# A first attention's scores as three single-pass products, with the work of four engines reordered around them

## What is computed

```python
x = x + tanh(g_xattn[0]) * L0_xattn(layernorm(x), ctx, ctx, mask, Wq, Wk, Wv, Wo)   # 32 query heads, 8 key heads of 128, rope, capped logits
x = x + tanh(g_ffn[0])   * L0_ffn(layernorm(x), ...)      # base matrix, 4 active low-rank experts, softmax router
x = x + tanh(g_xattn[1]) * L1_xattn(layernorm(x), ...)    # 8 heads of 8 within patches of 128
x = x + tanh(g_ffn[1])   * L1_ffn(layernorm(x), ...)      # 8 experts of 512x512, the best 2 of each row
```

```python
q, k = apply_rope(q), apply_rope(k)
logits = 30 * tanh(einsum('btkgd,bTkd->bkgtT', q, k) * 0.0883883 / 30)
weights = softmax(where(mask, logits, -1e30)); attn = einsum(weights, v); return attn @ Wo
```

## Time and profile before

| | |
|---|---|
| median of 3 runs | 913.25 us (911.86 to 913.34) |
| the profiled execution, own time | 913.61 us |
| its span in the profile | 911.8 us |
| busy: TensorE, VectorE, GpSimd, ScalarE | 96%, 67%, 46%, 36% |
| the 8 groups of the first attention | about 43 to 608 us |
| the experts' tiles | about 815 to 897 us |

### The profile page before, as it was taken

How to read it: one execution, slowest core, us unless ns; L and a number is a source line. 1 busy time by engine, 2 the same in 40 slices (tenths; PEclk the granted TensorE clock), 3 DMA queues, 4 the chain that set the end, 5 groups by cost and what they waited for, 6 DMA issues and landing times.

```text
span 911.8 us, 13908 instructions
## 1 busy us (share of the span) xinstructions
PE 874.1 (96%) x4786; PEld 708.4 (78%) x4786; DVE 608.6 (67%) x1059; ACT 326.2 (36%) x590; POOL 416.9 (46%) x423
## 2 busy tenths in 40 slices
PE   6899999999999999999999999999999999998992
PEld 4777877887877897787897787778789999557881
DVE  5876576456576537557536656768899886869445
ACT  4424124204214222412421411423266678542331
POOL 4463153253163225235315316334898865828651
PEclk9999999999999999999999999999999999999996
DMA  9010120002012002012001100203155230763448
GB/s 322 21 58 36 35 72 21 12 15 79 1 62 66 1 12 92 0 35 92 0 12 46 47 1 1 83 1 117 46 145 153 74 78 10 278 239 118 162 159 313
DMA packets 42344, 71.02 MB, mean 78 GB/s; under 512 B 7082, under 2 KB 14827, under 8 KB 42099
## 3 DMA queue, kind: packets, MB, share of 16 engines
q1 hardware_dynamic: 37170, 58.00, 19.8%
...
...
## 4 chain that ended last, share of the span: by engine, by line
PE 89%; DVE 5%; issue 2%; DMA 1%; ACT 1%; POOL 1%; ACTq 1%; SPq 0%; DVEq 0%; POOLq 0%
PE ps L1423 19%; PE ps L1425 19%; PE ps L1424 19%; PE ps L1548 6%; PE ps L1540 6%; PE ps L1681 6%; PE ps L1556 3%; PE ps L1669 3%; PE ps L1662 2%; DVE w_lo L1283 1%; PE ps L1808 1%; PE ps L1752 1%; PE ps L1471 1%; PE ps L1433 1%; DMA y_in<-y_rows 1%
## 5 line engine op out<-in xcount | busy, mean ns | idle before, releaser
L556 POOL TENSOR_TENSOR q_t<-rot_a,rot_b 128x512 f32<-128x512 f32 x64 | 82.6, 1291 | 149.8 <-DVE rot_b L1003 149.8
L1423 PE MATMUL ps<-xt_hi,wq_hi 128*128 128x512 f32 x256 | 107.6, 420 | 3.2 <-DVE rot_b L1003 3.1
L1001 DVE TENSOR_TENSOR rot_a<-ps,cos 128x512 f32<-128x512 f32 x80 | 55.1, 689 | 83.1 <-PE ps L1425 82.4
L1423 PE MATMUL ps<-wo_hi,at_hi 128*128 128x512 f32 x256 | 106.7, 417 | 0.4 <-DVE at_lo L1118 0.4
L790 ACT ACTIVATE ps<-ps 128x512 f32<-128x512 f32 x64 | 37.2, 582 | 178.7 <-PE ps L1540 178.7
L1425 PE MATMUL ps<-xt_hi,wq_lo 128*128 128x512 f32 x256 | 101.1, 395 | 0.0
L1424 PE MATMUL ps<-xt_lo,wq_hi 128*128 128x512 f32 x256 | 101.0, 394 | 0.0
L1425 PE MATMUL ps<-wo_hi,at_lo 128*128 128x512 f32 x256 | 100.2, 391 | 0.0
L1424 PE MATMUL ps<-wo_lo,at_hi 128*128 128x512 f32 x256 | 99.8, 390 | 0.0
L803 ACT ACTIVATE at_hi<-ps 128x512 fp32r<-128x512 f32 x64 | 38.2, 597 | 171.6 <-PE ps L1556 171.6
L1123 DVE TENSOR_TENSOR X<-ps,X 128x512 f32<-128x512 f32 x64 | 44.2, 690 | 74.4 <-PE ps L1425 74.1
...
## 6 DMA issues: line engine op xcount, KB each, us to landing
wq_raw<-in_wq SPq DMA_DIRECT2D x8, 1024.0 KB, 5.5
wo_raw<-in_wo SPq DMA_DIRECT2D x8, 1024.0 KB, 5.1
w_raw<-in_we SPq DMA_DIRECT2D x8, 1024.0 KB, 6.7
...
q_t<-in_ctx_t SPq DMA_DIRECT2D x2, 1024.0 KB, 10.0
...
```

What stands on the lines that cost most here:

```text
L556: nc.gpsimd.tensor_tensor(dst, rot_a[:, r % 2, :], rot_b[:, r % 2, :], ALU.add).then_inc(rope_ok, 1)
L1001: nc.vector.tensor_tensor(heads(rot_a[:, r % 2, :]), heads(bank), bcast(cos[:, :], 4), ALU.mult)
L1423: nc.tensor.matmul(dst, w_hi, x_hi, start=start and k == 0, stop=False)
```

## The change

It does four things.
1. The scores become a `product` of rounded and remaining parts. New tiles `q_hi`, `q_lo`, `k_hi`, `k_lo`. ScalarE rounds each rotated tile (`turned_hi`, ten a group); the remainders are made half on VectorE (`turned_lo` for r = 0 to 4) and half on GpSimd (r = 5 to 9), in place, since `q_t` and `k_t` now lie where `q_lo` and `k_lo` are (`over` gives a tile the place of the one allocated next). To make room, `wo_raw` lies where `wo_lo` is, so `load_wo` waits for the last output of the group before, and `v_ones` is narrower.
2. The queues are reordered: on TensorE `output(1)` comes before `scores(4)`, and an output does its eight products of the rounded rows before it waits for the remainders; ScalarE, GpSimd and SP as the diff shows.
3. The count and route operations move from before group 0 to between group 6 and group 7.
4. The experts' products come in fours (rounded, remaining rows, remaining weights), each with its own wait.

The diff, cut to its core:

```diff
...
-wo_raw = sb("wo_raw", [P, G, D])
 wo_hi = sb("wo_hi", [P, G, D], F32R)
+wo_raw = over("wo_raw", [P, G, D])
 wo_lo = sb("wo_lo", [P, G, D], F32R)
-q_t = sb("q_t", [P, G, N])
-k_t = sb("k_t", [P, N])
-v_ones = sb("v_ones", [P, B, 2, P + 4])
+q_hi = sb("q_hi", [P, G, N], F32R)
+q_t = over("q_t", [P, G, N])
+q_lo = sb("q_lo", [P, G, N], F32R)
+k_hi = sb("k_hi", [P, N], F32R)
+k_t = over("k_t", [P, N])
+k_lo = sb("k_lo", [P, N], F32R)
+v_ones = sb("v_ones", [P, B, 2, P + 2])
 e_w = sb("e_w", [P, 2, G * P])
...
+def turned_tile(r, queries, keys):
+    if r < 2:
+        return keys[:, r * HALF:(r + 1) * HALF]
+    half, head = divmod(r - 2, G)
+    return queries[:, head, half * HALF:(half + 1) * HALF]
...
             load_wv(g // 2)
-        sp.wait_ge(wo_lo_ok, CREDIT + G * g)
-        load_wo(g)
         sp.wait_ge(qp_mm, CREDIT + 8 * g)
         load_wq(g)
+        sp.wait_ge(wo_mm, CREDIT + B * g)
+        load_wo(g)
...
         gp.wait_ge(rot_ok, CREDIT + 10 * g + r + 1)
-        if r < 2:
-            dst = k_t[:, r * HALF:(r + 1) * HALF]
-        else:
-            half, head = divmod(r - 2, G)
-            dst = q_t[:, head, half * HALF:(half + 1) * HALF]
-        nc.gpsimd.tensor_tensor(dst, rot_a[:, r % 2, :], rot_b[:, r % 2, :], ALU.add).then_inc(rope_ok, 1)
+        nc.gpsimd.tensor_tensor(turned_tile(r, q_t, k_t), rot_a[:, r % 2, :], rot_b[:, r % 2, :], ALU.add).then_inc(rope_ok, 1)
+    def turned_lo(g, r):
+        gp.wait_ge(sh_ok, CREDIT + 10 * g + r + 1)
+        lo_part(turned_tile(r, q_lo, k_lo), turned_tile(r, q_t, k_t), turned_tile(r, q_hi, k_hi), sl2_ok)
     def group(g, p, odd, last=False):
-        for r in range(2, 10):
+        for r in range(2, 8):
             rope_sum(g, r)
-            if r < 2 + G:
-                wo_split(g, r - 2)
+            if r == 5:
+                turned_lo(g, 5)
+            if r >= 5:
+                wo_split(g, r - 5)
+        wo_split(g, 3)
+        rope_sum(g, 8)
+        turned_lo(g, 6)
+        turned_lo(g, 7)
+        turned_lo(g, 8)
+        rope_sum(g, 9)
+        turned_lo(g, 9)
         if last:
...
     row_hi_first(1)
+    def turned_hi(g, r):
+        ac.wait_ge(rope_ok, CREDIT + 10 * g + r + 1)
+        hi_part(turned_tile(r, q_hi, k_hi), turned_tile(r, q_t, k_t), sh_ok)
...
     row_hi_first(7)
+    turned_hi(0, 0)
+    turned_hi(0, 1)
     def group(g, p, odd, last=False, first=False):
-        for k in range(G):
-            wo_split(g, k)
         if not odd and not first:
...
+        for k in range(G):
+            turned_hi(g, 2 + k)
+            wo_split(g, k)
+        turned_hi(g, 6)
         weights(0)
         weights(1)
+        turned_hi(g, 7)
         for b in range(B):
...
                 weights(b + 2)
+            if b < 2:
+                turned_hi(g, 8 + b)
             if last and b >= B - 2:
...
                 wv_split(p + 1)
+        if not last:
+            turned_hi(g + 1, 0)
+            turned_hi(g + 1, 1)
...
     ac.wait_ge(route_in, 32)
-    nc.scalar.activation(tri[:, :], tri_raw[:, :], ACT.Copy).then_inc(tri_ok, 1)
+    nc.scalar.activation(tri[:, :], tri_raw[:, :], ACT.Copy).then_inc(kz_ok, 1)
     ac.wait_ge(c2_mm, CREDIT + B)
...
     nc.vector.memset(count[:, 0, :], 0.0).then_inc(prep_v, 1)
-    step = 4
+    step = 5
     def rotate(g, r):
...
+    def turned_lo(g, r):
+        ve.wait_ge(sh_ok, CREDIT + 10 * g + r + 1)
+        nc.vector.tensor_tensor(turned_tile(r, q_lo, k_lo), turned_tile(r, q_t, k_t), turned_tile(r, q_hi, k_hi).bitcast(F32),
+                                ALU.subtract).then_inc(sl_ok, 1)
...
     turned_first(7)
-    ve.wait_ge(prep_v, CREDIT + step)
-    for k in range(4):
-        nc.vector.scalar_tensor_tensor(count[:, k + 1, :], iota[:, :], active_f[:, k:k + 1], count[:, k, :],
-                                       ALU.is_equal, ALU.add).then_inc(prep_v, 1)
-        ve.wait_ge(prep_v, CREDIT + step + k + 1)
-    step += 4
-    nc.vector.tensor_scalar(absent[:, :], count[:, 4, :], 0.5, BIG, ALU.is_gt, ALU.mult).then_inc(prep_v, 1)
-    ve.wait_ge(gates_ok, CREDIT + 1)
-    nc.vector.tensor_tensor(route_1[:, :], log_prior[:, :], rb[:, :], ALU.add).then_inc(prep_v, 1)
-    ve.wait_ge(prep_v, CREDIT + step + 2)
-    nc.vector.tensor_scalar(absent2[:, :], absent[:, :], -BIG, None, ALU.add).then_inc(prep_v, 1)
-    ve.wait_ge(prep_v, CREDIT + step + 3)
-    nc.vector.tensor_tensor(route_bias[:, :], route_1[:, :], absent2[:, :], ALU.add).then_inc(prep_v, 1)
+    turned_lo(0, 0)
+    turned_lo(0, 1)
     ve.wait_ge(prep_mm, CREDIT + 1)
     nc.vector.tensor_scalar(cap[:, :], ps[:, 7, 0:P], 0.5, TINY, ALU.is_lt, ALU.mult).then_inc(prep_v, 1)
-    ve.wait_ge(prep_v, CREDIT + step + 5)
+    ve.wait_ge(prep_v, CREDIT + step)
     nc.vector.scalar_tensor_tensor(cap[:, :], maskf[:, :], BIG, cap[:, :], ALU.mult, ALU.add).then_inc(cap_ok, 1)
...
-        for r in range(2, 8):
+        rotate(g, 2)
+        for r in range(3, 8):
             rotate(g, r)
+            if r < 6:
+                turned_lo(g, r - 1)
         mask(0)
...
         add(B - 1)
+        if not last:
+            turned_lo(g + 1, 0)
+            turned_lo(g + 1, 1)
...
         group(g)
+    ve.wait_ge(prep_v, CREDIT + step)
+    for k in range(4):
+        nc.vector.scalar_tensor_tensor(count[:, k + 1, :], iota[:, :], active_f[:, k:k + 1], count[:, k, :],
+                                       ALU.is_equal, ALU.add).then_inc(prep_v, 1)
+        ve.wait_ge(prep_v, CREDIT + step + k + 1)
+    step += 4
+    nc.vector.tensor_scalar(absent[:, :], count[:, 4, :], 0.5, BIG, ALU.is_gt, ALU.mult).then_inc(prep_v, 1)
+    ve.wait_ge(gates_ok, CREDIT + 1)
+    nc.vector.tensor_tensor(route_1[:, :], log_prior[:, :], rb[:, :], ALU.add).then_inc(prep_v, 1)
+    ve.wait_ge(prep_v, CREDIT + step + 2)
+    nc.vector.tensor_scalar(absent2[:, :], absent[:, :], -BIG, None, ALU.add).then_inc(prep_v, 1)
+    ve.wait_ge(prep_v, CREDIT + step + 3)
+    nc.vector.tensor_tensor(route_bias[:, :], route_1[:, :], absent2[:, :], ALU.add).then_inc(prep_v, 1)
...
         def scores(b):
-            if b in (0, 4):
-                pe.wait_ge(rope_ok, CREDIT + 10 * g + 6 + b)
+            if b == 0:
+                pe.wait_ge(sl_ok, CREDIT + 5 * g + 5)
+                pe.wait_ge(sl2_ok, CREDIT + 5 * g + 1)
+            if b == 4:
+                pe.wait_ge(sl2_ok, CREDIT + 5 * g + 5)
             pe.wait_ge(e_ok, CREDIT + B * g + b - 1)
-            nc.tensor.matmul(ps[:, 2 + b % 2, :], k_t[:, b * P:(b + 1) * P], q_t[:, :, b * P:(b + 1) * P],
-                             start=True, stop=True).then_inc(s_mm, 1)
+            rows = slice(b * P, (b + 1) * P)
+            product(ps[:, 2 + b % 2, :], [(k_hi[:, rows], k_lo[:, rows], q_hi[:, :, rows], q_lo[:, :, rows])]).then_inc(s_mm, 1)
...
                 pe.wait_ge(wo_lo_ok, CREDIT + G * (g + 1))
+            pe.wait_ge(ah_ok, CREDIT + B * g + b + 1)
+            pe.wait_ge(x1_ok, CREDIT + B * g + b)
+            for n in range(G):
+                rows = at_hi[:, b % 2, n * P:(n + 1) * P]
+                nc.tensor.matmul(ps[:, 7, :], rows, wo_hi[:, n, :], start=n == 0, stop=False)
+                nc.tensor.matmul(ps[:, 7, :], rows, wo_lo[:, n, :], start=False, stop=False)
             pe.wait_ge(al_ok, CREDIT + B * g + b + 1)
-            pe.wait_ge(x1_ok, CREDIT + B * g + b)
-            product(ps[:, 7, :], [(at_hi[:, b % 2, n * P:(n + 1) * P], at_lo[:, b % 2, n * P:(n + 1) * P],
-                                   wo_hi[:, n, :], wo_lo[:, n, :]) for n in range(G)]).then_inc(wo_mm, 1)
+            for n in range(G):
+                end = nc.tensor.matmul(ps[:, 7, :], at_lo[:, b % 2, n * P:(n + 1) * P], wo_hi[:, n, :], start=False, stop=n == G - 1)
+            end.then_inc(wo_mm, 1)
...
             weighted(b)
-            if b + 2 < B:
+            if b == 2:
+                output(1)
+                scores(4)
+            elif b + 2 < B:
                 scores(b + 2)
...
                 next_keys(0, KT // 2, KT)
-            output(b - 1)
+            if b != 2:
+                output(b - 1)
             turn(b)
...
-    pe.wait_ge(kz_ok, CREDIT + 1)
-    pe.wait_ge(tri_ok, CREDIT + 1)
+    pe.wait_ge(kz_ok, CREDIT + 2)
     pe.wait_ge(sel_ok, CREDIT + 1)
...
         e = pe.value_load(of_tile_i[0:1, i:i + 1], min_val=0, max_val=EX - 1)
+        bank = ps[:, 4 + i % 4, :]
+        if i < EX:
+            pe.wait_ge(weh_ok, max(hi_count(KT * own + KT - 1) for own in range(i + 1)))
+        pe.wait_ge(gh_ok, CREDIT + i + 1)
+        pe.wait_ge(r_ok, CREDIT + i - 3)
+        for k in range(KT):
+            nc.tensor.matmul(bank, gx_hi[:, i % 2, k, :], w_hi[:, bass.ds(e, 1), k, :], start=k == 0, stop=False)
+        pe.wait_ge(glo_ok, CREDIT + i + 1)
+        for k in range(KT):
+            nc.tensor.matmul(bank, gx_lo[:, i % 2, k, :], w_hi[:, bass.ds(e, 1), k, :], start=False, stop=False)
         if i < EX:
...
                 pe.wait_ge(wel_v, CREDIT + by_v)
```

(18 more changed lines are left out.)

## The result

The changed kernel takes 931.9 us (median of 4 runs, 930.2 to 935.5), the kernel before 913.3 (median of 4 beside them). The ratio is 1.017, with a 95% interval of 1.012 to 1.021. Forecast 940.4, range 919 to 945: slower, as said, by two thirds of what was said.

A forecast was written before the change was run, and what follows sets the result against it. TensorE, busy 874.1 of 911.8 us, was taken to bound the kernel. Eight groups at +3.45 give +27.6; with -0.8 and +0.9 at the edges and experts -0.9, +26.8 on 913.6 makes 940.4 us, range 919 to 945.

The forecast's parts named there:

- scores: Each score's matmuls on TensorE shrink from 0.86 to 0.69 us: 0.17 saved, 1.36 us a group.
- tile 4, tile 5: TensorE stalls before query tiles 4 and 5, waiting for late rotations on VectorE: 0.9 and 1.15 us a group.
- scores(0): TensorE waits at a group's first scores for GpSimd's subtraction turned_lo(5): 0.65 us stall.
- weighted(0): TensorE waits at a group's first weighted sum for mask(0): 0.85 us stall.
- output(1): Later rotation 9 and turned_hi(9) delay at_hi(1), so TensorE waits: 0.5 us a group (0 to 1.0).
- output(2): TensorE waits for add(1), queued on VectorE behind mask(4): 0.85 us a group.
- the price of `turned_lo` on VectorE: Each such subtraction right behind a rotation, as GpSimd's rope sum starts, takes 1.83 us; bounds 0.61 and 1.83.
- row 34.07: Profile row: a VectorE operation on SBUF, 0.05 us ahead of GpSimd's rope sum, takes 1.63 us, ending 0.28 behind it.
- the rule beside it: Trainium skill: VectorE and GpSimd share an exclusive port, first issuer keeps it; as rival, GpSimd waits: 928 us, chance 0.17.
- 828.37: Profile row: a VectorE subtraction taking 2.31 us, ending 0.56 behind GpSimd's own, which starts at 828.81.
- this branch of the forecast: Main case, 940.4 us, chance 0.57: turned_lo on VectorE takes 1.83 us beside GpSimd's rope sum of 1.3.
- the chain over nine steps that ends at mask(0): Nine steps in a row from rotation 5 to mask(0), durations taken from rows, leading to the 0.85 us stall at weighted(0).

## Why the prediction was right in sign and range, and wrong in size

By its own steps, per group, and what the runs give:

| term | predicted | measured |
|---|---|---|
| scores | -1.36 | -0.99 (0.12 each for scores 0 to 2, none at scores(3), 0.17 and 0.18 in key-batches 4 and 5) |
| tile 4, tile 5 | +0.9, +1.15 | 0, 0 |
| scores(0) | +0.65 | +0.7 (0.49 removed, 0.21 left) |
| weighted(0) | +0.85 | +0.83 |
| output(1) | +0.5 | +0.23 removed (what is left at turn(1) is in the row of the scores) |
| output(2) | +0.85 | +0.88 |
| place of the tiles | not seen | +0.34 |
| group | +3.45 | +2.04 |

The measured terms sum to 1.99, within 0.05 of the 2.04.

**The step that failed** is the price of `turned_lo` on VectorE, "bounded by 0.61 ... and 1.83 ... I take 1.83, since its place is that of row 34.07". It measured 0.69, and 0.61 to the start of the next operation (118.02 to 118.63 in group 1), the lower bound: the sum on GpSimd waited. With it went the stalls of tiles 4 and 5, 2.05 us a group or 16.4 in all. Taking the decisive price from one row of another kind of operation, against the rule beside it, was the mistake; I had given that rule 0.17. The second row against it, 828.37, I misread. GpSimd was inside another instruction there when VectorE's began, and went on from it to its subtraction at 828.81:

```profile
827.84 0.96 POOL L677 DMA_INDIRECT rows_in<-h_rows,gather_i  x1 [0.30 <-PE ps L1808]
```

So VectorE did not come first to a free port in that row, and only 34.07 spoke against the rule. The rule's own sum, 928 us, is the nearest of the cases' figures. It priced the group at 1.75, and the profile has 2.04.

**Luck:** the 0.65 at scores(0). I had it from rotations that come late and a rope sum of 1.3 us. The rotations were not late, and 0.49 of the 0.7 us measured there is the rope sum that waited, which this branch of the forecast had at nothing; for that case I had put 1.0. The sizes of the scores' gain (-1.36 for -0.99) and of output(1) (+0.5 for +0.23) were off as well, and partly cancel.

**Right:** the chain over nine steps that ends at mask(0), and the queue orders: turned_hi(6) ahead of weights(0), mask(4) ahead of add(1). These two were named with their engine and price, and each came off when that one order was changed.

**Half right:** the count work. Ahead of the last group +1.0 for +0.9; at the start the gap fell by 0.35 us, from 3.07 to 2.72, of the 0.8 put there. The narrower v_ones was put at nothing, without a reason, and costs 2.7 us over eight groups. The experts' -0.9 (0 to -1.8) came to -1.4: the wait of 0.76 for `gx_lo` went, and the later ones stayed, as said. With these, the traces' terms are 16.3 + 1.0 - 0.35 - 1.4 = +15.6 us, against +26.8 forecast and 18.6 between the medians.
